# PSUM gates, moved scans, expert sums on TensorE, and GpSimd drains between indirect DMAs in a vision layer with a graph router

## The reference

```python
# token stage: 3x3 patches t (576 values a pixel), gated
h1  = relu(t @ W1 + b1);  s = sigmoid(h1 @ W2 + b2);  h = (t * s) @ W3 + b3
# sequence stage: linear recurrence over the nodes of an image
h = h + scan(layernorm(h) @ B) @ C + D * layernorm(h)
# router: graph attention over 16384 nodes and 262144 edges (src, dst)
e     = leaky_relu(a_src[src] + a_dst[dst])
alpha = segment_softmax(e, dst)
agg   = segment_sum(x[src] * alpha, dst) + b_gat      # plus each node's own loop
score = layernorm(agg).reshape(heads, experts).mean(heads)
g     = softmax over the best 2 of 4 experts
# experts
out = h + sum_e g[e] * (gelu(x @ W1[e] + b1[e]) @ W2[e] + b2[e])
```

## Time and profile before

| | us |
|---|---|
| three runs | 5581.59, 5600.37, 5612.91 (median 5600.37) |
| the profiled execution | 5620.4 |
| its span | 5618.7 |
| PE busy | 1949.2 (35%) |
| DVE busy | 2297.3 (41%) |
| ACT busy | 1167.0 (21%) |
| POOL busy | 2415.2 (43%) |
| of it L746, 2048 gathers | 2006.2 |
| idle time ahead of L746, ended by scans (L1570) | 1379.6 |
| POOL DMAs idle, ended by "issue" at L746 | 647.1 |

### The profile page before, as it was taken

How to read it: one execution, slowest core, us unless ns; L and a number is a source line. 1 busy time by engine, 2 the same in 40 slices (tenths; PEclk the granted TensorE clock), 3 DMA queues, 4 the chain that set the end, 5 groups by cost and what they waited for, 6 DMA issues and landing times.

```text
span 5618.7 us, 27673 instructions
## 1 busy us (share of the span) xinstructions
PE 1949.2 (35%) x7311; PEld 805.7 (14%) x7311; DVE 2297.3 (41%) x3986; ACT 1167.0 (21%) x1699; POOL 2415.2 (43%) x2473
## 2 busy tenths in 40 slices
PE   0611258591148173626442225151524344000000
PEld 0211113230013031212111102020202111000000
DVE  9899438480148172535435504040403010211237
ACT  0300025250024041313221203030313233000000
POOL 0000530547721707162535472726253553677571
PEclk9855579795569596857675657575757676555555
DMA  3100124241114132222213212121212122111023
GB/s 77 36 0 0 29 45 80 42 87 17 18 33 92 23 65 48 54 38 51 56 19 49 42 27 55 16 56 15 57 19 60 38 64 64 47 23 32 18 56 116
DMA packets 651776, 247.81 MB, mean 44 GB/s; under 512 B 552244, under 2 KB 632420, under 8 KB 649188
## 3 DMA queue, kind: packets, MB, share of 16 engines
q1 hardware_dynamic: 573700, 216.76, 16.6%
q0 software_dynamic: 77920, 29.29, 5.3%
HBM read 152.68 MB, written 91.71 MB: 43 GB/s over the span
## 4 chain that ended last, share of the span: by engine, by line
another core or an unknown queue 31%; PE 20%; DVE 14%; issue 14%; POOL 7%; DVEq 6%; ACT 3%; DMA 2%; SPq 1%; ACTq 0%; POOLq 0%
POOL ring L746 7%; DVE res L1233 3%; DVEq L1235 3%; PE ps L842 3%; PE ps L832 3%; PE ps L857 2%; PE ps L946 2%; DMA arena<-xnT 2%; DVE res L1566 1%; PE ps L968 1%; PE ps L957 1%; PE ps L883 1%; PE ps L891 1%; DVE msg L1554 1%
## 5 line engine op out<-in xcount | busy, mean ns | idle before, releaser
L746 POOL DMA_INDIRECT ring<-table,src_i x2048 | 2006.2, 980 | 2030.3 <-DVEq L1570 1379.6
L1578 DVE TENSOR_TENSOR arena<-arena 128x448 f32<-128x448 f32 x504 | 295.2, 620 | 596.8 <-issue 297.9
L842 PE MATMUL ps<-arena,w 64*128 64x448 f32 x896 | 265.6, 674 | 545.7 <-ACT arena L1048 300.7
L946 PE MATMUL ps<-arena 64*128 64x512 f32 x800 | 252.7, 748 | 518.5 <-DMA arena<-xnT 242.5
L1048 ACT ACTIVATE arena<-ps,tb 128x448 f32<-128x448 f32 x504 | 298.3, 631 | 620.2 <-remote 325.4
L1727 DVE TENSOR_TENSOR arena<-ps,arena 128x1024 f32<-128x1024 f32 x68 | 83.3, 1225 | 808.3 <-remote 609.0
L712 POOL DMA_INDIRECT ring<-keys_d,place x128 | 125.9, 984 | 630.3 <-DVEq L1190 589.8
L968 PE MATMUL ps<-ident,arena 128*128 128x128 f32 x800 | 140.7, 327 | 625.7 <-issue 414.3
L857 PE MATMUL ps<-arena,w 128*64 128x448 f32 x896 | 210.1, 592 | 350.8 <-issue 350.8
L1128 ACT ACTIVATE arena<-ps,arena 128x1024 f32<-128x1024 f32 x200 | 215.1, 1115 | 401.5 <-remote 266.8
L723 POOL DMA_INDIRECT adst_d<-res,place x128 | 137.6, 1075 | 352.6 <-DVEq L1515 215.7
(11 more groups left out here) (331 smaller groups left out, 3502.2 us busy)
## 6 DMA issues: line engine op xcount, KB each, us to landing
arena<-in_x SPq DMA_DIRECT2D x304, 110.0 KB
ring<-table,src_i POOLq DMA_INDIRECT x2048
partial<-res SPq DMA_DIRECT2D x16, 1536.0 KB
arena<-in_x SPq DMA_DIRECT2D x160, 140.0 KB
outputs_d<-arena SPq DMA_DIRECT2D x32, 512.0 KB
arena<-outputs_d SPq DMA_DIRECT2D x32, 512.0 KB
arena<-xnT SPq DMA_DIRECT2D x100, 128.0 KB
arena<-h_tok SPq DMA_DIRECT2D x50, 256.0 KB
```

What stands on the lines that cost most here:

```text
L746: g.indirect_dma_start(out=ring[k % 2][:, j - k * SC, :], out_offset=None, in_=table[0:GRAPH_NODES, :], in_offset=off(ap=src_i[:, j:j + 1] ...
L842: mm(bank(1 + (2 * i + z) % 3)[:, 0:CHUNK], w2[lower_upper(z), i * P:(i + 1) * P], h1[lower_upper(z), :], start=True, stop=True).then_inc( ...
L946: m = mm(hid[ee % 2][:, z * NT:(z + 1) * NT], fw1[lower_upper(z), ee, :], xf[q][lower_upper(z), :], start=True, stop=True)
L1578: v.tensor_tensor(r3(prod[:, t, :]), tap_view(s, t), r3(gate[t % 3]), ALU.mult)\
```

## The change

1. **Drains.** `rest(n)` puts a `drain` on GpSimd's queue ahead of every 16th (`BURST`) block gather, scatter and row gather, the latter up to number 1536 (`BURSTS_UNTIL`). That is 8 + 8 + 96 = 112 drains. The last 512 row gathers and the node rows have none.
2. **PSUM gates.** From front step 23 on (`PSUM_FROM`) `sigmoids` writes the gates in place, into the PSUM bank that it reads, and `gated` reads them there. ScalarE no longer waits for the product that frees a tile; TensorE waits for the product (`prod_done`) instead of the sigmoid (`gate_done`) before it writes the bank again.
3. **Moved scans.** From the same step the four `scan_states` of a step stand behind VectorE's wait for `std1_done`, right ahead of the instruction that makes u (L1638). Their rate is read from a PSUM word.
4. **Chunks and places.** The last chunk of 128 is cut into 96 and 32 (17 chunks, `SIZES`). Six scans follow front steps (31, 37, 43, 49, 54, 59; they were five: 31, 38, 44, 50, 56), five follow pairs (0, 8, 20, 31, 41; they were six: 1, 9, 17, 25, 33, 41), six come after the pairs. `EARLY_STEPS` is 17 for 18: ten scatters, not four, stand between chunks 0 and 1. SP loads back the scatters' rows ahead of the next pixels, not behind.
5. **Expert sums on TensorE.** In the node tail VectorE only multiplies by the gates (three buffers `yb`); four matmuls with the identity and a fifth for the residual add up in a PSUM bank, ScalarE copies it out, and SP stores one pair later.
6. **Node rows and gates.** Five node batches (24, 32, 32, 24, 16 rows; they were 40, 40, 32, 16), gathers throttled in groups of 4; `gate_fn` has three VectorE instructions fewer behind the wait for ScalarE (mean folded into the subtraction, the sum over heads taken before the scale).

```diff
+BURST = 16
+BURSTS_UNTIL = 1536
+PSUM_FROM = GRAPH_STEPS + 4
-NODE_BATCHES = [(0, 40), (40, 80), (80, 112), (112, 128)]
+NODE_BATCHES = [(0, 24), (24, 56), (56, 88), (88, 112), (112, 128)]
-SCAN_AFTER_STEP = {31: 0, 38: 1, 44: 2, 50: 3, 56: 4}
-SCAN_AFTER_PAIR = {1: 5, 9: 6, 17: 7, 25: 8, 33: 9, 41: 10}
+SCAN_AFTER_STEP = {31: 0, 37: 1, 43: 2, 49: 3, 54: 4, 59: 5}
+SCAN_AFTER_PAIR = {0: 6, 8: 7, 20: 8, 31: 9, 41: 10}
...
+            def rest(n):
+
+                if n % BURST == BURST - 1 and n < BURSTS_UNTIL:
+                    g.drain()
...
-                for j in range(k * SC, (k + 1) * SC):
-                    done = gather_group(k, j - k * SC)
+                for j in range(FROM[k], FROM[k] + SIZES[k]):
+                    rest(j)
+                    done = gather_group(k, j - FROM[k])
...
+        def gate_of(s, t):
+            return bank(1 + t % 3)[:, 0:CHUNK] if s >= PSUM_FROM else gate[t % 3]
...
-                wait(pe, S["gate_done"], TILES * s + 2 * i - 1)
+                wait(pe, S["prod_done"] if s >= PSUM_FROM else S["gate_done"], TILES * s + 2 * i - 1)
...
-                if j1 is not None:
-                    scan_states(j1, 1)
+                if j1 is not None and s < PSUM_FROM:
+                    scan_states(j1, 1, p_(3))
                 if j0 is not None:
                     dve.wait_ge(S["std1_done"], j0 + 1)
+                if s == PSUM_FROM:
+                    v.tensor_copy(rate_ps, p_(3))
+                if j1 is not None and s >= PSUM_FROM:
+                    v.drain()
+                    for z in range(2):
+                        scan_states(j1, z, rate_ps)
...
+            for hidx in range(2 * GRAPH_PAIRS):
+                k, z = OUT_PAIRS + hidx // 2, hidx % 2
+                o = bank(1 + hidx % 4)[:, 0:FF * CH]
+                pe.wait_ge(S["halves_gated"], hidx + 1)
...
+                for ee in range(EXPERTS):
+                    mm(o, ident[:, :], yb[hidx % 3][:, :, ee, :], start=ee == 0, stop=False)
+                mm(o, ident[:, :], hr[k % 2][:, z, :, :], start=False, stop=True).then_inc(S["halves_summed"], 1)
```

More of the change, by code:

```diff
@@ L91, with gathered @@
 SC = 128
-SCHUNKS = COLS // SC
+SIZES = [SC] * (COLS // SC - 1) + [96, 32]
+SCHUNKS = len(SIZES)
+FROM = [sum(SIZES[:k]) for k in range(SCHUNKS)]
+assert sum(SIZES) == COLS
+def gathered(k):
+    return 16 * sum(SIZES[k % 2:k + 1:2])
 NO_EDGES = EDGES + P
@@ L288, in build @@
         yT = [carve([2, NT]) for n in range(2)]
-        yb = carve([FF, EXPERTS, CH])
+        yb = [carve([FF, EXPERTS, CH]) for n in range(3)]
         yc = carve([FF, 2, CH])
@@ L299, in build @@
         r2 = carve([GK, EXPERTS - 1])
-        own = ring[0]
-        nrow = [ring_all[:, SC * TW + n * NB * RW:SC * TW + (n + 1) * NB * RW].rearrange("p (a b) -> p a b", b=RW)
-                for n in range(2)]
+        last_ring = (SCHUNKS - 1) % 2
+        own = ring[1 - last_ring]
+        nrow_at = [last_ring * SC * TW + n * NB * RW for n in range(2)]
+        nrow = [ring_all[:, n0:n0 + NB * RW].rearrange("p (a b) -> p a b", b=RW) for n0 in nrow_at]
         self_e = carve([P, HEADS])
@@ L356, in build, with node_count @@
         off = bass.IndirectOffsetOnAxis
+        def node_count(n, half, upto):
+            return 16 * sum(j // GROUP % 2 == half for a, b in NODE_BATCHES[n % 2:n + 1:2] for j in range(a, min(b, upto)))
         def x_loads(s):
@@ L697, in group_landed, with node_group @@
                 return done[n // GROUP % 2]
+            def node_group(n, j):
+                half = j // GROUP % 2
+                if j % GROUP == 0:
+                    of = n if j - 2 * GROUP >= NODE_BATCHES[n][0] else n - 1
+                    if of >= 0:
+                        pool.wait_ge(nrows[of % 2][half], node_count(of, half, j - GROUP))
+                return nrows[n % 2][half]
             def gather_group(k, i):
@@ L1810, in wide @@
                     return t.unsqueeze(3).broadcast_to([P, K, HEADS, EXPERTS])
-                dve.wait_ge(nrows[n % 2], 16 * sum(b - a for a, b in NODE_BATCHES[n % 2:n + 1:2]))
+                for half in range(2):
+                    dve.wait_ge(nrows[n % 2][half], node_count(n, half, k1))
                 seq(lambda: v.tensor_tensor(new, nr[:, :, 0:HEADS], self_e[:, ks_n, :], ALU.max),
```

182 lines of the change are left out of this document (108 added, 74 removed).

## The result

The changed kernel takes 5036 us (median; 4990 to 5069) against 5602 of the kernel before, a ratio of 0.897, 95% interval 0.891 to 0.903. So it is faster, as forecast, but by 566 us, not by 1400, and it lies 86 us above the top of the range. Executions of one kernel fall into a faster and a slower group, up to 3% apart, so ratios compare the faster ones, and the traces of e8, e9 and f4 are of slower ones. The profiled execution of after took 5019.9 us, its span is 5018.1.

What follows compares the result with a forecast made beforehand. TensorE's stall beside dense gathers was taken as the bound; once cured, POOL's queue: 1054 to the first gather, 1037 + 968 + 17 + 192 + 14 + 681, tail 254, sum 4217, forecast 4200 us, range 3880 to 4950.

Steps and rivals of the forecast that it cites:

- a drain: On GpSimd's queue: each drain was taken to cost 2 us, 192 us for the 96 among the row gathers.
- the stall doesn't build over 16 DMAs (20 us): TensorE beside gathers: the stall needs 15 us or more of back-to-back issue, so drains keep the layer at quiet pace.
- PSUM gates: nothing beside POOL's queue: Front steps: TensorE waits 0.6 to 0.7 us a step more for the last product, which costs nothing overall.
- moved scans: covered: Front steps: four scans cost VectorE 4.3 us a step, 26.1 in all, hidden by POOL's 189 us per chunk.
- the rule on VectorE: Front gathers: fewer instructions with two SBUF inputs would bring gathers nearer 1.28 us, the sum 54 us less.
- and amply with the experts: Beside the experts: scans come before POOL needs its ring, 12 pairs and a scan taking 160 us against POOL's 177.
- the last 512, behind the layer's end: Last row gathers, without drains: taken to run after the layer at 1.33 us each, 681 us.
- the tail: From the last row gather to the end: 254 us forecast, 68 less than the 322 of before.
- The start of the row gathers: The first row gather was forecast at 1054 us, against 1256.3 in the kernel before.
- Half a cure: Rival: TensorE slow for half of each burst, 40 to 50 us a chunk more, 4720 up to 4950 us; chance 0.16.
- drains are nearly free: Rival: drains cost 0, VectorE bounds the front at 184 us a chunk, 3880 to 3950 us; chance 0.06.
- the stall stays: Rival: 2 us pauses don't end the stall, drains and moved scans only add time, 5900 us; chance 0.15.

Runs made afterwards that it cites:

- e8: The changed kernel with its drains and moved scans (rate from PSUM), but gates in SBUF: 4862 us, 0.862.
- e9: The kernel before with drains among block gathers and scatters; at each 16th row gather a landing wait and 40 empty instructions: 5179 and 5282 us.
- f4: The changed kernel with gates in SBUF, state scans at old places, scans 8 pairs apart, drains up to row gather 1664, on a stalling chip: 4627 us, 0.826.
- e1: The kernel before with only the drains added, at the same places as in the changed kernel: 4511 us, 0.810.
- g1: The kernel before with drains among block gathers and scatters; a waited-for 128-column memset ahead of each of the first 1536 row gathers, no drains there: 4539 us, 0.809.
- g2: The changed kernel with gates in SBUF and the moved scans' rate read from SBUF instead of PSUM: 4686 us, 0.833.
- f3: The changed kernel, drains kept, with a tiny waited-for memset ahead of each of the first 1536 row gathers: 4553 us, 0.814.
- e6: The changed kernel with its drains, but gates in SBUF and the state scans at their old places in all steps: 4689 us, 0.841.
- e13: The changed kernel with gates in SBUF, state scans at old places, scans 8 pairs apart, drains up to row gather 1664, on chip C without the stall: 4324 us.
- e10: The kernel before, drains among block gathers and scatters, landing wait and three memsets at each 16th row gather, on chip C without the stall: 4398 us.
- e2: The changed kernel without any drain: 5810 us, 1.043.

## Why the prediction was wrong, by its own steps

**Right: the bound, and what drains do.** The stall of TensorE beside dense indirect DMAs was the 1.4 ms to be had. Drains take most of it away where nothing else is changed: 4511 us, front chunks 201 us apart for a forecast of 189. On a chip that hasn't the stall the kernel before takes 4081 on its own.

**Right in mechanism, off in size: a drain.** 2.5 us, taken as 2. A third of the difference between 189 and 201 comes from there (4 us a chunk), another from gathers that are 1.38 and not 1.35 apart beside a VectorE that really works, and part of the rest from starts across a drain, which VectorE holds up too (4.1 us in e1's mean, 3.7 in the rows above).

**Wrong: "the stall doesn't build over 16 DMAs (20 us)".** It does, behind some 10 to 15 us, when gathers are 1.25 to 1.27 apart (the pieces at 2156 to 2176 above). At 1.38 in the mean it does so far less (front steps of 22 to 33 us in e1, of 49 to 68 in the changed kernel), and with no two starts closer than 1.44 not at all (g1: 21.2). The step took the time since the last rest as the only thing that counts. The rows it rested on, seven or eight scatters in a row, had wider spacing too, 1.27 to 1.74 us between starts in the trace of before, and were over in some 11 us.

**Wrong, and the larger miss: "PSUM gates: nothing beside POOL's queue" and "moved scans: covered".** The cover was there; the step of 27.2 us (26.1 forecast) costs nothing in g2. But the edits change how often VectorE holds GpSimd up. The prediction had this link, in the paragraph on the rule on VectorE, and priced it only as shorter gathers, a gain of 54 us. It is the other way round: the gathers do come closer (1.38 to 1.27), and with that TensorE stalls again, some 350 to 410 us lost. That the operand does this is shown for the scans (g2), and that spacing alone gives it back for both (f3); how much of the gates' 200 us is their longer chain is not. It should also feed itself, since a stalled TensorE leaves VectorE idle and an idle VectorE lets the gathers come thicker; no run sets this apart.

**Wrong: "and amply with the experts".** A pair takes 11.1 us without a burst; beside drained gathers 12 pairs and a scan took 260 us in e6, over 19 us a pair. By the starts of chunks 10 to 13 the new places cost e6 133 us against e1, most of the difference between 0.841 and 0.810.

**Wrong: "the last 512, behind the layer's end".** Gathers 1536 to 1663 were still beside the experts: 251 us from this chunk to the next (3938.8 to 4190.0) in place of 170.

**Wrong: the tail.** 318 and not 254. Two waits of 22.62 and 23.97 us for TensorE's sums, 47 of the 64 us. The prediction costed the five matmuls at quiet durations, beside node rows that have no drains. It did the same for VectorE: the four instructions of a half, 2.9 us by the earlier trace rows, take 5.6 beside the node rows in e1 (L1737 at 4317.13 and at 4322.73), four times 1.40. On the chip without stall the tail of e13 is 4317.8 less 4066.8, the start of its last row gather, so 251 us. The term holds there, but not the gain of 68 us: with the old tail e10 has 4399.5 less 4123.7, so 276, and the edits save 25. The start of the row gathers is alike: 1055.7 in e13, for a forecast of 1054, and 1097.5 in the changed kernel, where POOL waits 83.0 us for VectorE ahead of a scatter and not 42.4 as in e13. Both terms took the stall as gone.

**The rivals.** Half a cure was the one that came, with 520 us and up to 750 over the forecast, and 801 in the trace. It was priced at 40 to 50 us a chunk; in the front it was 275 - 189 = 86. That drains are nearly free was wrong (2.5 us each), and so was that the stall stays.

## What to carry to other kernels

Where an engine that waits on nothing visible goes slow beside back-to-back indirect DMAs, space the DMAs evenly by a fraction of a microsecond before adding pauses, and look at what slows them already: work that gets in the DMA queue's way may be what keeps the rest running. Price a cure with nothing else changed, and again with each of the other edits, since edits that are free by busy time can change the pace of another engine. And measure such a case on more than one chip: here the kernel before takes 27% less on one of them, and each version with a cure that was timed there is slower than it.

## What the runs showed of the hardware

- TensorE beside indirect DMAs, on the chips where the kernel before takes about 5600 us: with 1.25 to 1.29 us from start to start it stalls after 10 to 15 us; with 1.38 in the mean (and rests) it keeps more of its pace (front steps of 22 to 33 us in e1); with 1.44 and more all of it, without a rest (21.2 us, g1). A pause of 1.7 us at each 16th helps a little (5179 and 5282 us), one of 2.8 to 2.9 us, by a drain or by memsets, much more (4511; 4518 and 4618).
- On the same chips VectorE too slows down beside such DMAs, with nothing to wait for: one instruction each 1.40 us, whatever its length (0.23 to 0.28 us in the rows at 5411 to 5415). GpSimd's own last 384 row gathers start 1.40 us apart 16 to 163 times in each of the sixteen traces that aren't of chip C, and not once in the four that are. So the stall looks like one of how instructions reach the engines, the second of the two places that the prediction named; but no run changes that, and the cause stays open.
- On one chip of four there is no such stall: 4081 us for the kernel before, and the quiet step of 21.2 us in e13, beside gathers 1.25 us apart in the median, 1.35 in the mean.
- VectorE's operands set GpSimd's pace: a gather took 1.37 us beside a state scan with its inputs in SBUF (g2), 0.944 with the rate in PSUM (e8); 128 gathers of a chunk took 141.72 and 125.06, and 120.98 beside a VectorE that mostly stands (e2).
- A GpSimd drain behind indirect DMAs costs 2.5 us over the usual gap of 0.30. Forty empty instructions on GpSimd's queue cost nothing that the trace shows.
- The rule of the Trainium skill that TensorE and ScalarE never wait on anyone for SBUF ("SBUF — State Buffer", "Who interferes with whom") isn't contradicted by a row, since no row names what TensorE waits for. TensorE stands still beside another engine's DMAs all the same, as the piece at 2171 to 2176 shows.
